# Cross-attention with layer norm: plain scores on 128 rows, q copied for two groups at a time, and an earlier eviction of the last q group

## The reference

```python
qs = (q @ wq).reshape(Bq, Lq, H, HD).transpose(0, 2, 1, 3)      # x is q: (4, 2048, 512)
ks_ = (k @ wk).reshape(Bq, Lk, H, HD).transpose(0, 2, 1, 3)     # context: (4, 77, 512)
vs = (v @ wv).reshape(Bq, Lk, H, HD).transpose(0, 2, 1, 3)
scores = jnp.einsum('bhqd,bhkd->bhqk', qs, ks_) / jnp.sqrt(jnp.float32(HD))
scores = jnp.where(mask[:, None, :, :], -jnp.inf, scores)
attn_w = jax.nn.softmax(scores, axis=-1)
attn = jnp.einsum('bhqk,bhkd->bhqd', attn_w, vs)
out = attn.transpose(0, 2, 1, 3).reshape(Bq, Lq, H * HD) @ wo + q
mu = jnp.mean(out, axis=-1, keepdims=True)
var = jnp.mean((out - mu) ** 2, axis=-1, keepdims=True)
return (out - mu) / jnp.sqrt(var + EPS) * gamma + beta
```

## Time and profile before

| | |
|---|---|
| median of 3 runs | 643.23 us (642.08 to 643.83) |
| the profiled execution | 644.06 us |
| its span in the profile | 642.3 us |
| mean granted TensorE clock | 0.993 |
| busy share of the span | PE 96%, PEld 74%, DVE 82%, ACT 79%, POOL 77% |
| DMA queue of SyncE | 90.01 MB, 48.5% of 16 engines' span |
| copies qd<-qn | 240 of 128 KB, issue to landing 2.4 us (median) |
| chain that ended last | PE 69%, DVE 7%, SyncE's queue 7%, DMA 6%, POOL 5%, issue 4%, ACT 2% |

### The profile page before, as it was taken

The page is one execution under the profiler, slowest core; times in us unless marked ns, Lnnn a source line. Parts: engine busy times, 40 slices in busy tenths (PEclk is TensorE's granted clock), DMA queues, the critical chain, the costliest instruction groups (busy, mean ns, idle before and its releaser), DMA issues.

```text
span 642.3 us, 12825 instructions
## 1 busy us (share of the span) xinstructions
PE 614.2 (96%) x3840; PEld 478.0 (74%) x3840; DVE 529.8 (82%) x1008; ACT 506.4 (79%) x1558; POOL 493.4 (77%) x639
## 2 busy tenths in 40 slices
PE   7999998999999999999999999999999999998995
PEld 5777687777868878786877878786876778786763
DVE  5876687788879888887888888888888788888887
ACT  4867778888978888888987888897887888786750
POOL 6366556787987979798996979799796969687784
PEclk9999998999999999999999999999999999999998
DMA  8843346173562718355362827355371735635103
GB/s 296 222 136 89 98 145 182 53 211 115 139 180 88 213 50 228 102 160 168 108 183 71 226 82 196 132 138 161 115 196 51 209 119 142 220 87 144 50 34 115
DMA packets 57363, 90.82 MB, mean 141 GB/s; under 512 B 11984, under 2 KB 15056, under 8 KB 57296
## 3 DMA queue, kind: packets, MB, share of 16 engines
q1 hardware_dynamic: 57296, 90.01, 48.5%
HBM read 39.53 MB, written 16.78 MB: 88 GB/s over the span
## 4 chain that ended last, share of the span: by engine, by line
PE 69%; DVE 7%; SPq 7%; DMA 6%; POOL 5%; issue 4%; ACT 2%; POOLq 0%; ACTq 0%; DVEq 0%
PE bank L383 24%; PE bank L477 17%; SPq L290 7%; PE bank L429 6%; PE bank L419 6%; DMA qd<-qn 5%; PE bank L405 5%; PE bank L450 4%; PE bank L455 2%; PE bank L433 2%; PE bank L361 2%; POOL pn L907 1%; DVE pr L736 1%; DVE sm L749 1%; DVE nm L742 1%
## 5 line engine op out<-in xcount | busy, mean ns | idle before, releaser
L595 ACT ACTIVATE pr<-pr,nm 128x77 f32<-128x77 f32 x1024 | 269.8, 348 | 51.9 <-DVE nm L742 49.9
L907 POOL TENSOR_TENSOR pn<-pr,rec 128x512 f32<-128x512 f32 x128 | 134.8, 1053 | 97.1 <-DVE rec L751 92.2
L736 DVE SCALAR_TENSOR_TENSOR pr<-msk,bank 128x308 f32<-128x308 uint8 x256 | 110.8, 469 | 42.7 <-PE bank L419 32.5
L383 PE MATMUL bank<-xh,wqh 128*128 128x512 f32 x256 | 105.0, 410 | 2.5 <-DVE ql L724 2.3
L749 DVE TENSOR_REDUCE sm<-pr 128x8 f32<-128x616 f32 x128 | 99.8, 780 | 8.3 <-ACT pr L595 7.1
L477 PE MATMUL bank<-woh,ah 128*128 128x512 f32 x256 | 105.2, 411 | 1.4 <-DVE al L758 1.4
L742 DVE TENSOR_REDUCE nm<-pr 128x8 f32<-128x616 f32 x128 | 101.8, 795 | 4.4
L557 ACT ACTIVATE ptr<-bank 128x512 f32<-128x512 f32 (+1 forms) x256 | 95.5, 427 | 9.8 <-PE bank L429 9.6
L477 PE MATMUL bank<-wol,ah 128*128 128x512 f32 x256 | 102.3, 400 | 0.0
L477 PE MATMUL bank<-woh,al 128*128 128x512 f32 x256 | 102.1, 399 | 0.0
L383 PE MATMUL bank<-xh,wql 128*128 128x512 f32 x256 | 100.7, 393 | 0.0
(11 more groups left out here) (81 smaller groups left out, 1000.2 us busy)
## 6 DMA issues: line engine op xcount, KB each, us to landing
qd<-qn SPq DMA_DIRECT2D x240, 128.0 KB, 2.4
xraw<-xT SPq DMA_DIRECT2D x58, 256.0 KB, 3.4
xres<-x SPq DMA_DIRECT2D x58, 256.0 KB, 2.9
out<-y SPq DMA_DIRECT2D x56, 256.0 KB, 2.1
ptr<-xT SPq DMA_DIRECT2D x6, 256.0 KB, 8.7
zt<-x SPq DMA_DIRECT2D x6, 256.0 KB, 4.0
out<-zt SPq DMA_DIRECT2D x6, 256.0 KB, 2.0
kd<-kh SPq DMA_DIRECT2D x8, 154.0 KB, 3.8
```

The costliest lines, as they stand in the source:

```text
L383: last = nc.tensor.matmul(misc_bank(("q", i))[:], w[:, k, m * P:(m + 1) * P], s[:, blk % 2, k, :], start=(k == 0 and n == 0), stop=(k == K ...
L595: last = nc.scalar.activation(s, s, ACT.Exp, bias=nm[:, t % 2, h:h + 1], scale=1.0)
L736: nc.vector.scalar_tensor_tensor(out=pr[:, 4 * g:4 * g + 4, :], in0=msk[:, b % 2, t % TB, :].unsqueeze(1).broadcast_to([P, 4, LK]), scalar ...
L907: nc.gpsimd.tensor_tensor(pn[:, half, 0:4, :].rearrange("p s (e k) -> p (s e) k", e=2), pr[:, hs, 0:KM], rec[:, t % 2, hs].unsqueeze(2).br ...
```

## The change

There are four edits.

1. In the plain way the fourth matmul takes all 128 rows of q and of `kd` (second half). For this the first 64 rows of `kd`, u = 1, must stay zero for batch 0 as long as plain scores run. So `pair_k` leaves batch 0 out of its second copy, and two new copies (`pair_k0`, one for two groups, 64 x 2 x 154) bring it in SyncE's turn 4, after the plain scores of these groups.
2. `qd` is laid out by half u first and then by group, and `double_q` copies two neighbouring groups by one DMA: four copies of 64 rows by 1024 columns (256 KB) for two groups. In a regular block it is called twice, for groups 0 and 1 and for groups 2 and 3. Each call waits for the scores and the eviction of the second of its groups. The doubled q of a pair has one semaphore, so the scores of both groups wait for the whole pair.
3. For block 1 the pairs are copied in turns 2 and 4 (DOUBLES); the second waits for all plain scores.
4. ScalarE evicts the last group of q (`keep_q(t + 4)`, t % 4 == 3) ahead of the transposed probabilities `keep_pt(t - 1, 0)`, and no longer behind them.

```diff
--- before.py
+++ after.py
@@ -36,7 +36,7 @@
 VALUES = {t: STEP_OF[t - 5] for t in range(5, T - 4, 4)}
 LAG = 6
 
-DOUBLES = {1: 4, 2: 5, 3: 6, 4: 7}
+DOUBLES = {2: 4, 4: 6}
 
 V_AT = {1: (1,), 3: (2, range(0, 2)), 4: (2, range(2, 4))}
 V_KEPT = {2: 1, 5: 2}
@@ -125,7 +125,7 @@
         with ExitStack() as second:
             second.enter_context(nc.sbuf_tensor("below_kt", [P, 6 * D], f32))
             kt_sb = second.enter_context(nc.sbuf_tensor("kt_sb", [P, NB, NG, PW], f32r))
-        qd = sb("qd", [P, NG, 2, D], f32r)
+        qd = sb("qd", [P, 2, NG, D], f32r)
         qn = sb("qn", [P, NG, D], f32r)
         ah = sb("ah", [P, NG, D], f32r)
         al = sb("al", [P, NG, D], f32r)
@@ -171,7 +171,8 @@
         d_xr = [sem(f"d_xr{i}") for i in range(XR)]
         d_y = [sem(f"d_y{i}") for i in range(YS)]
         d_kd = [sem(f"d_kd{g}") for g in range(NG)]
-        d_qd = [sem(f"d_qd{g}") for g in range(NG)]
+        d_k0 = [sem(f"d_k0{i}") for i in range(2)]
+        d_qd = [sem(f"d_qd{i}") for i in range(2)]
         d_end, d_xe = sem("d_end"), sem("d_xe")
 
         p_k, p_v, p_q, p_s, p_tp, p_pv, p_o = (
@@ -269,26 +270,30 @@
             def pair_k(g):
 
                 sp.wait_ge(a_k, 4 * g + 4)
-                for u in range(2):
-                    sp.dma_start(kd[0:64, g, u].bitcast(f32), kh[64 * u:64 * u + 64, g, :, u * PW:(u + 1) * PW].bitcast(f32)
-                                 ).then_inc(d_kd[g], 16)
+                sp.dma_start(kd[0:64, g, 0].bitcast(f32), kh[0:64, g, :, 0:PW].bitcast(f32)).then_inc(d_kd[g], 16)
+                sp.dma_start(kd[0:64, g, 1, 1:NB].bitcast(f32), kh[64:128, g, 1:NB, PW:GW].bitcast(f32)).then_inc(d_kd[g], 16)
                 sp.wait_ge(v_k, 4 * g + 4)
                 for j in range(2):
                     sp.dma_start(kd[64 + 32 * j:96 + 32 * j, g, 0, :, j * LK:(j + 1) * LK].bitcast(f32),
                                  kt[32 * j:32 * j + 32, g, :, j * LK:(j + 1) * LK].bitcast(f32)).then_inc(d_kd[g], 16)
 
+            def pair_k0(g):
+
+                sp.wait_ge(p_s, NG * PLAIN + g + 2)
+                sp.dma_start(kd[0:64, g:g + 2, 1, 0].bitcast(f32), kh[64:128, g:g + 2, 0, PW:GW].bitcast(f32)).then_inc(d_k0[g // 2], 16)
+
             def double_q(i):
 
                 blk, m = i // 4, i % 4
                 if blk > 1:
-                    sp.wait_ge(p_s, NG * (4 * blk - 1) + m + 1)
-                elif m == NG - 1:
+                    sp.wait_ge(p_s, NG * (4 * blk - 1) + m + 2)
+                elif m > 0:
                     sp.wait_ge(p_s, NG * (PLAIN + 1))
-                sp.wait_ge(a_qh, i + 1)
+                sp.wait_ge(a_qh, i + 2)
                 for u in range(2):
                     for v in range(2):
-                        sp.dma_start(qd[64 * v:64 * v + 64, m, u].bitcast(f32), qn[64 * u:64 * u + 64, m].bitcast(f32)
-                                     ).then_inc(d_qd[m], 16)
+                        sp.dma_start(qd[64 * v:64 * v + 64, u, m:m + 2].bitcast(f32), qn[64 * u:64 * u + 64, m:m + 2].bitcast(f32)
+                                     ).then_inc(d_qd[m // 2], 16)
 
             for k in range(KT):
                 sp.dma_start(wq_raw[:, k, :], w_v(wq)[:, k, :]).then_inc(d_wq[k], 16)
@@ -309,11 +314,14 @@
             for t in range(T + LAG):
                 if t >= 1 and t + 9 < 4 * NBLK:
                     load_slice(t + 9)
+                if t == PLAIN:
+                    pair_k0(0)
+                    pair_k0(2)
                 if t in DOUBLES:
                     double_q(DOUBLES[t])
                 if t % 4 == 3 and 3 < t < T - 4:
-                    for i in range(t + 1, t + 5):
-                        double_q(i)
+                    double_q(t + 1)
+                    double_q(t + 3)
                 if t == 5:
                     sp.wait_ge(p_v, 3)
                     for o in range(XR):
@@ -408,15 +416,16 @@
                         nc.tensor.matmul(o[:, 0:PW], qk[blk][:, g, r * P:(r + 1) * P], kt[:, g, t // TB, :],
                                          start=False, stop=False)
                         nc.tensor.matmul(o[:, 0:GW], qk[blk][:, g, r * P:(r + 1) * P], kh[:, g, t // TB, :], start=False, stop=False)
-                        nc.tensor.matmul(o[:, PW:GW], qk[blk][64:128, g, r * P:(r + 1) * P], kd[64:128, g, 1, t // TB, :],
+                        nc.tensor.matmul(o[:, PW:GW], qk[blk][:, g, r * P:(r + 1) * P], kd[:, g, 1, t // TB, :],
                                          start=False, stop=True).then_inc(p_s, 1)
                         continue
                     if r == 0 or t == PLAIN + 1:
-                        pe.wait_ge(d_qd[g], 64 * blk)
+                        pe.wait_ge(d_qd[g // 2], 64 * blk)
                         if blk == 1:
+                            pe.wait_ge(d_k0[g // 2], 16)
                             pe.wait_ge(d_kd[g], 64)
                     for u in range(2):
-                        last = nc.tensor.matmul(o[:, u * PW:(u + 1) * PW], qd[:, g, u, r * P:(r + 1) * P],
+                        last = nc.tensor.matmul(o[:, u * PW:(u + 1) * PW], qd[:, u, g, r * P:(r + 1) * P],
                                                 kd[:, g, u, t // TB, :], start=False, stop=(u == 1))
                     last.then_inc(p_s, 1)
 
@@ -575,7 +584,7 @@
                 if blk == 2:
                     act.wait_ge(p_s, NG * PLAIN + m + 1)
                 if blk >= 2:
-                    act.wait_ge(d_qd[m], 64 * (blk - 1))
+                    act.wait_ge(d_qd[m // 2], 64 * (blk - 1))
                 keep(qk[blk][:, m, :], misc_bank(("q", i))[:]).then_inc(a_qh, 1)
 
             def keep_pt(t, half):
@@ -662,10 +671,10 @@
                     keep_x(8)
                 if t in VALUES:
                     keep_a(VALUES[t])
+                if t % 4 == 3:
+                    keep_q(t + 4)
                 if t >= 1:
                     keep_pt(t - 1, 0)
-                if t % 4 == 3:
-                    keep_q(t + 4)
                 exps(t, 1)
 
             keep_pt(T - 6, 1)
```

## The result

The changed kernel takes 652.9 us (median of 4 runs, 651.07 to 653.43) against 642.8 us (4 runs): the ratio is 1.0151, 95% interval 1.0126 to 1.0176. It is 1.5% slower, where I had forecast 635.5 us. The profiled execution took 653.4 us with a span of 651.6 us, so 9.3 us more than the span before.

The account below looks back on a forecast made before the run. TensorE was nearly always busy; its largest wait, 10.3 us, was for doubled q copies. 644.06 - 4.9 (those waits) - 3.5 (beginning) = 635.7 us, 634.8 for the median; forecast 635.5, range 632 to 639 (8 in 10: 630.5 to 642).

Parts of the forecast that it names:

- Edit 2, second pair: Regular blocks, copies for groups 2 and 3: first issue about 430.45, landing 436.75, a wait of 0.35 us per block.
- Group 2 waits for group 3's bytes: Regular blocks: group 2 needs the whole pair and wants weights at 436.67, not 437.03; counted within 0.35 us per block.
- First pair hidden: Regular blocks: copies for groups 0 and 1 land at 431.9 to 432.5, before group 0 loads at 432.59; no wait.
- The rate: Regular burst of q copies: 202 GB/s seen, 230 at a full share, about half the rate on 128 partitions.
- The fit: Copy rule weighed but rejected: about 2 us fixed plus bytes at 436 GB/s, so 256 KB lands 2.6 us after issue.
- Edit 1, the plain scores: Plain scores: a group falls from 0.86 to 0.50 us, 7.2 us for five tiles, about 4.8 us of it kept.
- The rule: Plain scores: weight loads overlap matmuls in flight only in another row group, so 128-row loads would gain nothing; rejected.
- The beginning: Start of the kernel: 4.8 - 0.65 - 0.6 = 3.5 us saved, bounds 0 and 7.2.
- Edit 4: ScalarE evicts q from 429.76, not 430.39; probabilities start 0.58 us later, costing 0.58 us once in the beginning.
- Rival D: Slower: regular blocks wait 0.4 us at group 0 and 1.25 at group 2, giving 651.7 us; chance 0.08.
- full-share rate: Regular burst with DMA engines fully busy: 230 GB/s, so 1.14 us per 256 KB copy, against 1.30 at 202 GB/s.
- Rival E, the clock: Near 98 to 100 us: longer TensorE idling could add a low-clock stretch, 1.5 us more; no chance of its own.

Follow-up runs that it names:

- followers held: Changed kernel, but SyncE waits until the second pair has landed before issuing the output write and the residual and x loads: 641.4 us; on single copies with edits 1 and 4, 640.0.
- mixed kernels: Changed kernel with groups 2 and 3 copied singly, groups 0 and 1 still a pair: 639.3 us; with SyncE also waiting for the last copy, 640.2 us.
- the pairs alone: Edits 2 and 3 alone on the kernel before, plain scores and ScalarE's order unchanged: 671.5 us, ratio 1.0446.

## Why the prediction was wrong

- **Edit 2, second pair: wrong, and this is most of the error.** Of the 17.4 us between forecast and median the waits are 13.4 (18.0 against 4.6), the beginning 2.9 and the clock 1.7, which come to 18.0. I had its first issue 6.3 us ahead of the landing of its last copy. In the block above it is issued at 430.60 + 5.05 = 435.65 (its place in the burst, by the trace) and lands at 443.1, 7.5 us later, for a need 6.3 us later. The step that failed is the landing, "1.75 us from issue to landing" and then 1.14 us for each copy. With the followers held the same step takes 6.8 us (430.7 to 437.48). So of the 1.2 us that the sum left out, some 0.7 are the followers' and the rest is the copies' own. The sum took the landing of the copies of before as a property of a copy. It was one of the situation: 0.65 us between issues, and no other traffic until the last was nearly through. I put 0.35 us of wait per block and got 18.0 / 13 = 1.4.
- **The sentence that hid it.** I wrote that SyncE's long issues "now fall into slack: four issues take 2.6 us, their transfers 4.6". That slack is what lets the output and two loads in behind the copies. The 16 issues had kept them away. I counted the followers nowhere; holding them is worth 11.5 us with the pairs and nothing without.
- **Group 2 waits for group 3's bytes: seen, too cheap.** The mechanism was in the text, at 0.35 us per block or 4.6 us in all; by itself it costs 6.3 us on top of the waits that were there. The two causes are not independent: the wait for the whole pair takes the cover away, then what the followers add is paid in full. With groups 2 and 3 copied singly neither shows.
- **First pair hidden: nearly right.** Group 0 waits 3.5 us in all, where I had put nothing, and the pair for groups 0 and 1 alone costs nothing (639.3 us).
- **The rate: right.** 212 to 225 GB/s, near the 202 to 230 I had counted with, and with half the bytes the waits vanish. The fit that I took from the Trainium skill, DMA: Bandwidth & Descriptors, "Anatomy of one DMA", stands there for DMAs issued from GpSimd; here SyncE issues them, and copies of 256 KB landed in 4.6 us (median) and not in 2.6.
- **Edit 1, the plain scores: right.** 0.50 us a group, 4.6 us earlier at tile 5 (4.8 forecast). The rule of the Trainium skill that spoke against it (TensorE: Matmul & The Clock Gate, "Part 3: Packing small matmuls") is not borne out: in the plain group above the weight loads of 128 rows start 0.11 to 0.14 us apart, beside matmuls of 128 rows that take 0.23 to 0.34 us.
- **The beginning: wrong in the changed kernel,** where 0.6 of 3.5 us were left. The number fits edits 1 and 4 alone (measured 2.8 us, and 3.0 without edit 4), but that is at least in part luck, since with edit 1 alone the profile has 0.8 us of it at tile 8. SyncE's chain is longer with copies of 256 KB: 3.21 us for four issues and 2.69 for the two behind them, where before 2.38 and 1.34. That accounts for some of the loss only: with edit 1 alone and copies of 128 KB, ScalarE still waits 4.91 us for the same load of x.
- **Edit 4: cost nothing that can be measured (0.6 us forecast), and probably gave more than I had credited.** It does nothing for single copies, while without edits 1 and 4 the pairs cost 28 us.
- **Rival D** had the places and nearly the prices: 0.4 us per block at group 0 and 1.25 at group 2, measured 0.27 and 1.11. Its time, 651.7 us, was as near as it is in part by luck: its waits were 3.5 us too long, its beginning 2.9 us too good, and it had nothing for the clock (1.7 us). I gave it 0.08. Its cause was only half there: I had let it rest on a lower rate and the first pair's rest, not on other traffic. I held the full-share rate to be nearer "since SyncE no longer paces the queue"; the same fact should have raised D.
- **Rival E, the clock,** came true for 1.7 us more in the beginning (3.4 us against 1.7) and 1.7 us near 595 us.

The Trainium skill, DMA: Bandwidth & Descriptors, "Queues, rings and completion order", says that each DMA engine takes a queue's descriptors in the order of the ring, but that a later one may finish its write before an earlier one. By the first half alone DMAs issued behind a copy could not delay it; the second leaves room for it, without a price. The trace shows that they do: 5.6 us from issue to landing with followers, 5.0 without, and 11.5 us over the kernel. Where exactly they meet (the ports, the writes under way) no run here shows.

Left open: where edit 1 wins its 3 us, why the beginning of the mixed kernels loses what their waits gain, and how much of the differences of 1 to 2 us between the kernels near 640 us is the beginning, which moves by itself (over the profiles the first scores start between 1.2 us later and 0.5 us earlier than before).

## What to carry to other kernels

The time from issue to landing is read from copies in the crowd that they had. When copies are merged, ask who is issued behind them and now comes earlier, and let each consumer wait for its own bytes: merge only where the first reader is far off. An issue that looks like pure cost can be the spacing that keeps other traffic away from a transfer that is waited for. An edit that measures nothing alone can matter beside another (the earlier eviction seems to save the pairs some 7 to 9 us of waits), so parts have to be tried together too.

## What the hardware showed that I had not expected

- SyncE's issues are not all alike: one of the changed kernel takes 461 to 2124 ns, median 598. In the block above the fourth of each pair is the long one, 1.96 and 1.26 us, issued while the three ahead of it are under way. With copies of 128 KB single issues of up to 1.88 us occur too. What holds them back no run here shows.

```profile
L295 SPq DMA_DIRECT2D qd<-qn x120: 461/598/2124, 44.5 to 587.2; - x120
```

- The length of a wait does not decide what the clock does. In the pairs alone waits of 1.91 and 2.29 us were followed by some 3.4 us at 1.2 GHz, which costs 1.7 us more, and one of 2.30 us by none; in the changed kernel two waits of 1.33 and 0.37 us near 594 us were, and one of 1.78 us at 143 us was not. Longer waits met a low stretch more often: four of the 13 of the pairs alone that last over 1.7 us, one of all 21 behind 120 us in the changed kernel.
- The order in which four copies between the same two halves are issued changed the kernel a little, and not always the same way: with single copies 0.4 to 0.7% faster (0.9882 and 0.9917 against 0.9957), with pairs and followers held 0.4% slower (1.0009 against 0.9969).
